# A four-layer vision Mamba block on one core: who adds the directions' sum to y in the two columnwise directions

## The reference, cut to what matters

```python
# u: (384, 64*64) after projection, convolution and SiLU; four orders k of the same positions
xs = [rows, columns, rows reversed, columns reversed]
delta = softplus(dt_w[k] @ dts[k] + dt_bias[k])
for each position t of order k:
    h = exp(delta[t] * A[k]) * h + delta[t] * B[k, :, t] * xs[k][t]      # 16 states per channel
    y[k][t] = sum over states of h * C[k, :, t]
y = y[0] + y[1] + y[2] + y[3] (each put back in row order) + u * sum of D[k]
out = x + out_proj(layernorm(y) * silu(z))
```

## Time and profile before

| | us |
|---|---|
| median of 3 runs | 28529.37 |
| profiled execution | 28593.1 |
| its span | 28591.4 |
| TensorE matmul busy (share) | 27059.4 (95%) |
| VectorE busy | 25875.7 (91%) |
| ScalarE busy | 18929.7 (66%) |
| GpSimd busy | 23415.0 (82%) |
| DMA, mean | 94 GB/s |

### The profile page before, as it was taken

How to read it: one execution, slowest core, us unless ns; L and a number is a source line. 1 busy time by engine, 2 the same in 40 slices (tenths; PEclk the granted TensorE clock), 3 DMA queues, 4 the chain that set the end, 5 groups by cost and what they waited for, 6 DMA issues and landing times. The chain is left out here.

```text
span 28591.4 us, 600844 instructions
## 1 busy us (share of the span) xinstructions
PE 27059.4 (95%) x242880; PEld 20043.6 (70%) x242880; DVE 25875.7 (91%) x24430; ACT 18929.7 (66%) x37728; POOL 23415.0 (82%) x10688
## 2 busy tenths in 40 slices
PE   8999998998999999899899999989989999998998
PEld 6776775774677677577467767757746776775774
DVE  8998997997899899899789989979978998997997
ACT  6775775774677577577467757757746775775774
POOL 7996995994799699599479969959947996995994
PEclk9999999999999999999999999999999999999999
DMA  3332332331333233233133323323313332332331
GB/s 106 102 101 80 105 105 80 106 110 44 101 104 100 82 103 105 80 109 108 45 100 105 99 82 102 105 80 108 108 45 100 105 99 82 102 105 80 108 108 45
DMA packets 3552030, 2679.50 MB, mean 94 GB/s; under 512 B 3255348, under 2 KB 3258636, under 8 KB 3294584
## 3 DMA queue, kind: packets, MB, share of 16 engines
q1 hardware_dynamic: 489912, 2628.56, 25.9%
q10 hardware_dynamic: 3059328, 12.24, 6.2%
HBM read 2541.99 MB, written 111.15 MB: 93 GB/s over the span
## 5 line engine op out<-in xcount | busy, mean ns | idle before, releaser
L971 POOL TENSOR_TENSOR regB<-regB,regA 128x1024 f32<-128x1024 f32 x9216 | 21517.9, 2376 | 618.8 <-ACT carry L838 607.4
L932 DVE TENSOR_TENSOR_SCAN regB<-regB,carry,ps 128x512 f32<-128x512 f32 x16128 | 19137.1, 1257 | 243.6 <-PE ps L730 215.8
L849 ACT ACTIVATE regB<-regB,a_neg 128x512 f32<-128x512 f32 x18432 | 12184.1, 710 | 0.6 <-issue 0.2
L730 PEld LDWEIGHTS ps<-regA,regB 64*128 64x128 f32 x147456 | 8999.2, 188 | 3536.0 <-issue 2923.7
L730 PE MATMUL ps<-regA,regB 64*128 64x128 f32 x147456 | 10741.4, 285 | 104.7 <-DVE regB L932 59.1
L744 PE MATMUL ps<-ident,regB 128*128 128x128 f32 x73728 | 10082.7, 280 | 229.1 <-POOL regB L971 163.3
L744 PEld LDWEIGHTS ps<-ident,regB 128*128 128x128 f32 x73728 | 7905.5, 141 | 1407.4 <-POOL regB L971 397.9
L838 ACT ACTIVATE carry<-regB 128x2 f32<-128x2 f32 x9216 | 1888.8, 205 | 6151.6 <-DVE regB L932 5617.7
L961 POOL TENSOR_TENSOR regB<-regB,u 128x512 f32<-128x512 f32 x1152 | 1635.0, 1419 | 1972.2 <-DVE regB L915 1972.2
L932 DVE TENSOR_TENSOR_SCAN regB<-regB,ps 128x512 f32<-128x512 f32 x2304 | 2617.4, 1200 | 229.2 <-PE ps L730 193.8
L705 PE MATMUL ps<-regB,dt_w 13*128 13x512 f32 (+1 forms) x2304 | 1274.5, 633 | 171.8 <-SPq L667 171.8
(11 more groups left out here) (103 smaller groups left out, 13630.7 us busy)
## 6 DMA issues: line engine op xcount, KB each, us to landing
regA<-c SPq DMA_DIRECT2D x1536, 1024.0 KB, 4.7
regA<-eye SPq DMA_DIRECT2D x384, 2048.0 KB, 7.7
regA<-x_in SPq DMA_DIRECT2D x16, 1536.0 KB, 13.5
x_keep<-regA SPq DMA_DIRECT2D x8, 3072.0 KB, 17.6
regA<-x_keep SPq DMA_DIRECT2D x16, 1536.0 KB, 13.9
regB<-xd SPq DMA_DIRECT2D x128, 192.0 KB
regB<-w_in_in SPq DMA_DIRECT2D x28, 576.0 KB, 11.5
xd<-regB SPq DMA_DIRECT2D x64, 192.0 KB
```

What stands on the lines that cost most here:

```text
L730: mm = nc.tensor.matmul(b.rearrange("p (t s) -> p s t", s=2), dtuT[at, up, q, :], diag[at, cp, q, g], start=True, stop=True)
L849: nc.scalar.activation(decays[:, g % 2, s], dt[:, up, :], ACT.Exp, scale=a_neg[:, c[0], d, 2 * g + s:2 * g + s + 1]).then_inc(a_made, 1)
L932: nc.vector.tensor_tensor_scan(ring[:, g % RING, s, way], decays[:, g % 2, s, way], b[:, s, way], 0.0 if begun else carry[:, d, at:at + 1] ...
L971: nc.gpsimd.tensor_tensor(ring[:, g % RING], ring[:, g % RING], c_all[:, g], ALU.mult).then_inc(g_made, 1)
```

## The change

In directions 1 and 3 (`ADD_ON_DVE`) TensorE's identity matmul by `y_acc` and ScalarE's copy back are left out. The four transposes of `turn_y` open the PSUM group themselves, so the bank holds this direction's y alone, and VectorE adds it to `y_acc` in place (`add_y`), behind the scans of pair 6 of the next unit (`DVE_Y`). Directions 0 and 2 stay as they are.

```diff
+DVE_Y = 6
+ADD_ON_DVE = (1, 3)
@@ start_y (TensorE)
                         pe.wait_ge(yT_kept, U + 1)
+                        if k in ADD_ON_DVE:
+                            return
@@ turn_y (TensorE)
-                                                  start=False, stop=q == QS - 1, is_transpose=True)
+                                                  start=c[0] in ADD_ON_DVE and q == 0, stop=q == QS - 1,
+                                                  is_transpose=True)
@@ VectorE
+                    def add_y(c, d, up):
+
+                        k, n, _, S = c
+                        if k not in ADD_ON_DVE:
+                            return
+                        dve.wait_ge(y_mm, unit(c, d) + 1)
+                        dve.wait_ge(y_kept, unit(c, d) - NDB + 1)
+                        y = in_order(y_acc, k, d, n)
+                        nc.vector.tensor_tensor(y, y, as_chunk(ps[:, Y_BANK + up, :], k), ALU.add).then_inc(y_kept, 1)
...
                                 scans(this, d, g)
                                 if nxt and g == DVE_DT:
                                     make_dt(*nxt, par_of(nxt[0], par, this, nxt[1]))
+                                if g == DVE_Y and (old := behind(this, before, d, 0, PAIRS)):
+                                    add_y(old[0], old[1], par_of(old[0], par, this, old[1]))
                     chunks(dve, step)
+                    add_y(LAST, NDB - 1, NDB % 2)
```

## The result

| | before | changed |
|---|---|---|
| median, us | 28523.1 (4 runs) | 28896.2 (4 runs) |
| ratio | 1 | 1.013 (95%: 1.0115 to 1.0145) |
| profiled span, us | 28591.4 | 28911.2 |

The changed kernel is 1.3% slower: 373 us by the medians, 320 us by the two profiled executions. The forecast was 28768 us (+239), the range 28620 to 29040. The measured time lies inside the range and on the side that was forecast; the forecast was 0.64 to 0.75 of the loss.

The account below looks back on a forecast made before the run. The prediction took TensorE to bound column order at 20.56 us a unit. Layers 0 and 1 (+146 us), layer 2 (+115) and scan tails (-22) sum to +239 on 28529.4: 28768 us, range 28620 to 29040.

Parts of the forecast that it names:

- The bound: In column order TensorE bounds the unit at 20.56 us, with GpSimd at 20.10 and VectorE at 20.07.
- The worth by itself: Leaving out TensorE's identity matmul in column order alone gains 0.46 us a unit, down to GpSimd's 20.10.
- ScalarE's copy worth nothing: Leaving out ScalarE's 1062 ns copy back in column order gains nothing by itself, the engine being busy 340 of 460 us.
- The wait of the add costs nothing: VectorE's add waits for the turned y of the unit before, with several us of cover.
- The add's size: VectorE's added instruction in column order takes 1.00 us of pitch a unit, with ends at 0.61 and 1.80.
- The two constructions: Pitch of VectorE's strided add: 0.94 us from a memory limit of 1.68 ns an element, or 1.09 from ScalarE's stride surcharge.
- The directions: A column-order direction takes 503.1 us after the change, from 21 units of 21.07 and 3 of 20.2; layer 2's direction 1 509.3.
- The tail: At each scan's end 1.8 us of matmul goes and a 1.0 us add replaces ScalarE's 1.06 us copy: -22 us.
- Stride free: Rival: the step of 64 costs VectorE's add nothing, pitch 0.61 us, +35 us, 28564 us; chance 0.11, free or nearly.
- Shared limit: Rival: the add's strided read and write share the memory limit, 1.88 us, pitch 1.80, +700 us, 29229 us; chance 0.10.
- TensorE's clock: Rival: TensorE, left with waits in column order, drops to 0.83 of its clock; about 29710 us; chance 0.04.
- Shorter scans: Rival: without strides beside them VectorE's scans fall from 1.17 to 1.12 us, -200 us, 28329 us; chance 0.04.

Follow-up runs that it names:

- 28383.7 us run: The changed kernel with VectorE's add left out, the results of directions 1 and 3 dropped and the semaphore still counted: 28383.7 us, ratio 0.9928 to the kernel before.

## Why the prediction was right, point by point

- **The bound.** Right in kind. TensorE ran 459 of 460 us in column order and bound it; taking its matmul away is worth 206 us, when nothing is given in return. The 20.07 us floor of VectorE came out unchanged (28383.7 us run). The worth by itself, 0.46 us a unit, was too much: 206 us over 576 units are 0.36. The steady unit before is 20.56 us in layers 0 and 1 but 20.37 in layer 2, and one unit in three gives back less. GpSimd's 20.10 as the next bound isn't borne out: with TensorE relieved the steady unit is 20.08 us.
- **ScalarE's copy worth nothing.** Not refuted: 18 us between the runs with and without it, within their intervals.
- **The wait of the add costs nothing.** Right: 74.3 us of idle time in all, and only at the ends of scans, where ScalarE's copy waited before.
- **The add's size.** The term that was mis-sized. It was 0.61 us for a contiguous add, right (0.58 from its start to the next scan's, 0.60 by the ruler; the add itself took 665 ns, so line 915's 692 was not quite a lower end), plus 0.39 for the stride; the stride costs 0.62. The two constructions, 0.94 and 1.09 of pitch, carried over what TensorE and ScalarE showed, and both of those stride on one side only. The one-sided case is there as computed, 1.02 us against 1.042 and 1.046. The two-sided one was a rival at 1.88 us, with a chance of 0.10; the truth lies between, at 1.283, and depends on how far apart the two sides lie. 0.21 us x 576 = 121 us turn the forecast of +239 into +360, against 320 in the profiled executions and 373 in the medians. Two of the signs that the prediction named for itself failed with this term: the add at 1.0 to 1.1 us, and the ruler at 21.0 to 21.1.
- **The directions.** Direction 1 of the first scan came to 507.1 us, 503.1 + 24 x 0.21 = 508.1 by the prediction's own sum. That is closer than its working, and partly luck. The adds of a direction's last two units fall behind the next ruler, so 22 stand between these two and not 24, and the second unit, with no add in it, took 20.23 us where 20.2 were reckoned with one.
- **The sum over all scans.** The ruler, read in the two profiled executions over all 12 scans, says where the 320 us lie: directions 1 and 3 lost 169 and 170 us (direction 3 without its last unit), where the prediction's +261, corrected by the 121 above, gives 382 for both. Directions 0 and 2 won 23 and 16, and the stretches between the scans lost 20. Why the row-order directions got shorter stays open: no step of the change explains it. The ten runs of the kernel with the contiguous add lie up to 52 us apart, so it may be chance.
- **The tail.** -1.8 us a scan was forecast. From ScalarE's last copy to the next stage it came to 4.05 - 5.51 = -1.5. But what stands just before it takes that back. From the ruler's last row to the end of the scans it was 29.66 us and is 31.23, with two adds in it (2.44 us by the ruler's price) and only 0.87 us of relief. From that row to the next stage the first scan took 2126.62 - 2087.60 = 39.02 us before and takes 2150.00 - 2110.01 = 39.99; over the 12 scans this stretch lost 6.6 us. The forecast had -22 for the tails and some +6 for the last units, so it was some 23 us too low here.
- **The rivals.** Stride free: refuted for the add as written, but real for the same elements in another order, and then near the price it was given (+23 us for +35, not clear of no change). Shared limit: its 1.88 us refuted, but its reason, that a read and a write of the same place both stride, is what the one-sided rows lacked. TensorE's clock: 1.00 at 90% busy in column order, so no loss. Shorter scans: refuted, 20.07 us without TensorE's and ScalarE's strides beside them.
- **The Trainium skill's rules.** That crossing to a new 16-byte line costs in SBUF (SBUF — State Buffer, Specifications) agrees with these runs: 665 ns in runs of 8 elements, 1042 with each element far from the one before. That the plain mode works with odd strides (VectorE: DVE Perf Modes, Mode 1× (REGULAR) — the baseline) is true of the result and not of the time.

## What to carry to other kernels

Work moved from the bounding engine to another is worth no more than the gap between the two, here 0.49 us a unit at the steady pace and 0.36 over all units, and costs what it takes beyond it; measure the gap with a ruler instruction before moving anything. Before an operation with a long step is moved, turn its loops so that SBUF is walked in runs of neighbours and PSUM takes the step: that alone gave 0.6% on the kernel before, which the move itself could not. A price read from an operation that strides on one side is not the price of one that strides on both, least of all in place. And the length of an instruction is not its price: the ruler is.

## What the runs showed of the hardware that I had not expected

- On VectorE a float32 add of 128x512 out of PSUM takes 665 ns with contiguous SBUF operands, 1042 with the read at a step of 64 elements, 1046 with the write, and 1283 with both at the same place within the step; 1075 with the two 4 elements apart within it, 1045 with 8. In the time of a unit the strided read costs 0.39 us and the strided write 0.29.
- A step of 64 elements in PSUM cost nothing on VectorE's read (665 ns), TensorE's write (594 ns a record) and ScalarE's read (576 ns).
- VectorE's scans, at 18.84 us for 16, did not become shorter when TensorE's and ScalarE's strided accesses were taken away: the unit took the 20.07 us of row order.
